# Cross-attention on one core: the next batch's memory blocks move from SP's DMA queue to ScalarE's

## What is computed

```
mp    = memory @ W_mem.T                        # (2048, 1024) a batch
attn  = softmax(x @ mp.T / sqrt(1024))
ctx   = attn @ mp
gate  = sigmoid(concat(x, ctx) @ W_gate.T + b_gate)
out   = rmsnorm(x + gate * ctx) * norm_w
```

## Time and profile before

| what | us |
|---|---|
| median of 3 runs | 1560.95 |
| profiled execution, its own time | 1556.9 |
| its span | 1555.1 |
| PE busy | 1528.3 (98%) |
| DVE busy | 1080.3 (69%) |
| ACT busy | 549.0 (35%) |

### The profile page before, as it was taken

The page is one execution under the profiler, slowest core; times in us unless marked ns, Lnnn a source line. Parts: engine busy times, 40 slices in busy tenths (PEclk is TensorE's granted clock), DMA queues, the critical chain, the costliest instruction groups (busy, mean ns, idle before and its releaser), DMA issues.

```text
span 1555.1 us, 21137 instructions
## 1 busy us (share of the span) xinstructions
PE 1528.3 (98%) x6720; PEld 1262.0 (81%) x6720; DVE 1080.3 (69%) x1502; ACT 549.0 (35%) x919; POOL 33.3 (2%) x72
## 2 busy tenths in 40 slices
PE   7999999999999999999999999999999999999997
PEld 5888888888888878888788888888888888888886
DVE  5654758777777864467446754567555899989987
ACT  4232342222222352244222432234222554444443
POOL 0000000000000000000000000000000001100011
PEclk9999999999999999999999999999999999999999
DMA  9997526333332786757584666757748645555553
GB/s 197 235 241 178 127 88 175 113 113 113 108 108 95 171 214 158 180 142 189 154 208 131 166 166 172 181 139 196 189 133 282 215 181 191 194 197 197 198 198 120
DMA packets 213399, 262.63 MB, mean 169 GB/s; under 512 B 19312, under 2 KB 136048, under 8 KB 213104
## 3 DMA queue, kind: packets, MB, share of 16 engines
q1 hardware_dynamic: 213360, 262.20, 59.8%
HBM read 170.39 MB, written 89.65 MB: 167 GB/s over the span
## 4 chain that ended last, share of the span: by engine, by line
PE 44%; DMA 3%; DVE 1%; issue 1%; ACT 1%; SPq 1%; POOL 0%; ACTq 0%; DVEq 0%; POOLq 0%
PE bank L1604 25%; PE bank L1753 19%; DMA prob_scratch<-prob 2%; DMA region_f<-in_ctx 1%; DMA region_f<-prob_scratch 1%; ACT prob L807 1%; DVE region_l L311 0%; SPq L453 0%; DVE region_n L311 0%; DVE max_part L1232 0%; DVE region_f L1328 0%; SPq L509 0%; ACT region_t L818 0%; ACT region_l L825 0%; POOL mean_sq L693 0%
## 5 line engine op out<-in xcount | busy, mean ns | idle before, releaser
L1604 PE MATMUL bank<-region_n,region_l 128*128 128x512 f32 x1536 | 353.6, 389 | 2.6 <-DVE region_l L311 2.6
L1604 PE MATMUL bank<-region_t,region_l 128*128 128x512 f32 x1536 | 353.7, 389 | 2.2 <-DVE region_l L311 2.1
L1604 PEld LDWEIGHTS bank<-region_t,region_l 128*128 128x128 f32 x1536 | 288.0, 188 | 63.8 <-issue 4.2
L1604 PEld LDWEIGHTS bank<-region_n,region_l 128*128 128x128 f32 x1536 | 288.2, 188 | 63.1 <-DVE region_l L311 2.9
L1604 PE MATMUL bank<-region_t,region_n 128*128 128x512 f32 x960 | 220.2, 392 | 11.6 <-DVE region_t L311 11.6
L1604 PEld LDWEIGHTS bank<-region_t,region_n 128*128 128x128 f32 x960 | 181.4, 189 | 49.9 <-DVE region_t L311 12.0
L825 ACT CAST region_l<-bank 128x512 fp32r<-128x512 f32 x128 | 75.0, 586 | 329.2 <-DVE bank L1261 329.0
L1261 DVE STREAM_TRANSPOSE bank<-region_f 128x512 f32<-128x512 f32 x128 | 88.7, 716 | 102.5 <-DMA region_f<-prob_scratch 100.3
L311 DVE TENSOR_TENSOR region_t<-region_f,region_t 128x1024 fp32r<-128x1024 f32 (+2 forms) x77 | 110.5, 1466 | 67.3 <-ACT region_t L711 60.5
L1645 PE MATMUL bank<-region_t,region_l 128*128 128x512 f32 x576 | 135.7, 389 | 0.0
L1645 PEld LDWEIGHTS bank<-region_t,region_l 128*128 128x128 f32 x576 | 108.1, 188 | 22.4
(11 more groups left out here) (87 smaller groups left out, 1427.6 us busy)
## 6 DMA issues: line engine op xcount, KB each, us to landing
region_f<-in_ctx SPq DMA_DIRECT2D x128, 256.0 KB, 5.6
prob_scratch<-prob SPq DMA_DIRECT2D x128, 256.0 KB, 2.7
region_f<-prob_scratch SPq DMA_DIRECT2D x128, 256.0 KB, 4.3
region_f<-in_x SPq DMA_DIRECT2D x64, 256.0 KB, 6.1
region_f<-in_x SPq DMA_DIRECT2D x128, 128.0 KB, 2.7
region_f<-in_x SPq DMA_DIRECT2D x16, 1024.0 KB, 4.9
out<-region_f SPq DMA_DIRECT2D x31, 512.0 KB, 2.6
q_scratch<-prob SPq DMA_DIRECT2D x8, 1024.0 KB, 6.3
```

Of the source, the lines that this page charges most:

```text
L1604: mm = nc.tensor.matmul(dst, lhs(a), rhs(b), start=first and n == 0, stop=last and n == len(PASSES) - 1)
```

## The change

All loads of the next batch's memory blocks leave SP's stream. ACT issues them, on its own DMA queue: an mt block at the end of a step's work, after `q_split` (steps 1 to 4; in batch 0 steps 2 to 4, two of them after step 2), mn 0 after step 5, mn 1 at the end of step 6, mn 2 in step 7 between the last `pt_split` and the exponentials, mn 3 in step 7 after `q_split`. The split of mn 2 moves: ACT does it at the end of step 7, DVE at the start of step 8. The split of mn 3 moves behind the pieces of step 8. SP's loop over the steps becomes uniform: queries, exchange, store.

```
@@ sync
-            load_next_mt(0, 0)
-            step_sp(2)
-            for j in range(1, MB):
-                load_next_mt(0, j)
-            rest_of_batch(0)
-            with sp.Fori(1, NB - 1) as b:
-                for j in range(MB):
-                    if j < 2:
-                        step_sp(b * UPB + 1 + j)
-                    load_next_mt(b, j)
-                rest_of_batch(b)
+            with sp.Fori(2, (NB - 1) * UPB + 1) as i:
+                step_sp(i)
@@ scalar
+            def next_mt(b, j):
+                act.wait_ge(mn_ready, b * MB)
+                load_mt(act, b, j)
+            def next_mn(b, j):
+                if j == 0:
+                    act.wait_ge(mt_t, b * MTS + MTS)
+                else:
+                    act.wait_ge(mt_ready, b * MTS + HPJ * (j + 1))
+                load_mn(act, b, j)
             def step_act(i, ...):
                 for g in range(MB):
-                    if mn_of is not None and g >= MN_EARLY:
-                        act.wait_ge(av_done, (mn_of * UPB - 1) * MB + g + 1)
-                        mn_split(mn_of, g)
                     pt_split(i, g)
+                if mn_of is not None:
+                    mn_split(mn_of, MB - 1)
+                if mn_next is not None:
+                    next_mn(mn_next, 2)
...
+                if mt_of is not None:
+                    next_mn(mt_of, 1)
                 if mn_next is not None:
-                    for g in range(MN_EARLY):
+                    next_mn(mn_next, 3)
+                    for g in range(MB - 1):
                         act.wait_ge(av_done, (mn_next * UPB - 1) * MB + g + 1)
                         mn_split(mn_next, g)
...
             with act.Fori(1, NB - 1) as b:
-                with act.Fori(1, 6) as u:
-                    step_act(b * UPB + u)
+                for j in range(MB):
+                    step_act(b * UPB + j + 1)
+                    next_mt(b + 1, j)
+                step_act(b * UPB + MB + 1)
+                next_mn(b + 1, 0)
                 rest_of_batch(b)
@@ vector, step_dve
+                if mn_of is not None:
+                    mn_split(mn_of, MN_EARLY)
                 dve.wait_ge(px_loaded, (i + 1) * (16 * NQ))
...
                     pt_split(i, g)
-                    if mn_of is not None and g >= MN_EARLY:
-                        mn_split(mn_of, g)
                 if softmax:
                     unit_max(i + 1)
+                if mn_of is not None:
+                    mn_split(mn_of, MB - 1)
```

More of the change, by code:

```diff
@@ L335, in build, with load_mt, load_mn @@
         NGEV = 6
+        def load_mt(eng, b, j, dst=None):
+            load_quadrants(eng, b_in[j] if dst is None else dst, mem[b, BANK * j:BANK * (j + 1), :], C, mt_loaded[j])
+        def load_mn(eng, b, j):
+            v = b_in[MN_SLOT[j]].rearrange("p (s c) -> p s c", s=TPB)
+            for q in range(NQ):
+                r = M // NQ * q + P * j
+                eng.dma_start(v[SQ * q:SQ * (q + 1)],
+                              mem[b, r:r + P, :].rearrange("(s i) c -> i s c", i=SQ)).then_inc(mn_loaded[j], 16)
         block = ctx.enter_context(nc.Block())
@@ L444, in _ @@
             load_zraw(2, 1)
[L445 to L454, removed]
             sp.wait_ge(w7_ready, W7[S1])
-            load_mt(0, 0, mt0_raw[0])
+            load_mt(sp, 0, 0, mt0_raw[0])
             with sp.Fori(0, NPAIR - 3) as p:
@@ L477, in _ @@
             sp.wait_ge(z_ready, NPROD * NPAIR - 1)
-            load_mt(0, 1)
+            load_mt(sp, 0, 1)
             store_zx(p, 1, slice(0, D), EV_C21, zx_stored[2])
             sp.wait_ge(z_ready, NPROD * NPAIR)
-            load_mt(0, 2)
+            load_mt(sp, 0, 2)
             store_zx(p, 0, slice(BANK, D), EV_C12, zx_stored[1])
             sp.wait_ge(mt_t, HPJ)
-            load_mt(0, 3, mt0_raw[3])
+            load_mt(sp, 0, 3, mt0_raw[3])
             store_zx(p + 1, 0, slice(0, BANK), EV_C11, zx_stored[0])
             sp.wait_ge(mt_ready, HPJ * 2)
-            load_mn(0, 1)
+            load_mn(sp, 0, 1)
             store_zx(p + 1, 1, slice(0, D), EV_C21, zx_stored[2])
@@ L490, in _ @@
             store_zx(p + 1, 0, slice(BANK, D), EV_C12, zx_stored[1])
[L492 to L496, removed]
             def exchange(unit, first=False):
@@ L522, in _ @@
                 sp.wait_ge(zx_stored[i], 16 * NPAIR)
-            load_mn(0, 0)
+            load_mn(sp, 0, 0)
             exchange(0, first=True)
             sp.wait_ge(mt_ready, HPJ * 3)
-            load_mn(0, 2)
+            load_mn(sp, 0, 2)
             sp.wait_ge(mt_ready, MTS)
-            load_mn(0, 3)
+            load_mn(sp, 0, 3)
             def load_q_after_next(i):
@@ L538, in step_sp @@
                 store_am(i)
[L540 to L561, removed]
             sp.dma_start(q_third, q_dram[3]).then_inc(q_first_loaded[3], 16)
@@ L888, in rest_of_batch @@
                 step_act(b * UPB + 8, mn_of=b + 1)
-            with act.Fori(2, 6) as u:
-                step_act(u)
+            step_act(2)
+            next_mt(1, 0)
+            next_mt(1, 1)
+            step_act(3)
+            next_mt(1, 2)
+            step_act(4)
+            next_mt(1, 3)
+            step_act(5)
+            next_mn(1, 0)
             rest_of_batch(0)
             with act.Fori(1, NB - 1) as b:
-                with act.Fori(1, 6) as u:
-                    step_act(b * UPB + u)
+                for j in range(MB):
[3 more added lines that the diff above has]
+                next_mn(b + 1, 0)
                 rest_of_batch(b)
```

## The result

The changed kernel takes 1581.46 us (median of 4 runs, 1581.19 to 1582.14) against 1560.72 before (4 runs). The ratio is 1.0145, 95% interval 1.0133 to 1.0157: slower by 20.7 us. The forecast was 1558.0 in a range of 1557.0 to 1567.0. It was wrong in sign and outside its range. The profiled execution took 1581.58 us with a span of 1579.8, 24.7 more than the span before.

A forecast was written before the change was run, and what follows sets the result against it. PE was taken as the bound, busy for 98% of the span. The terms -2.60 - 0.34 + 0 = -2.94 us took 1560.95 to 1558.0 us; the range of 8 in 10 was 1557.0 to 1567.0.

The forecast's parts named there:

- d = 2.0: Loaded steps of attention: each exchange of weights comes back 2.0 us late, below the 2.8 at which PE stands.
- part (6): Loads running beside the exchange: claimed each exchange late by 2.0 us, between 0 and 5.1, unseen by PE.
- the prize: All PE idle time the change could win back in attention: 2.94 us, 0.19% of the time.
- the five gaps: Late starts of PE ahead of scores phases: 1.07, 0.21, 0.96, 0.13 and 0.57 us.
- Part (1): Splits of mn 2 and 3 leave the pieces of step 8: three late starts close, -2.60 us.
- Part (2): The queue of twelve mt DMAs ahead of the queries' load goes: -0.34 us.
- Part (3): Issuing 32 DMAs a batch on ACT: 0.51 us each, 2.0 a block, in ACT's idle time, no cost to PE.
- Part (4): ACT's waits before mt, mn 0 and mn 1 loads: only a cast queued behind mn 0's, cost nothing.
- The upper bound of 2.7: Exchange beside one block: lateness if the block uses 2.4 us of idle DMA time and otherwise goes first.
- the 5.5 of reserve: Settled step of attention: one exchange can come 5.5 us late before PE stands.
- Rival A: Loaded steps: contention makes every exchange over 2.8 us late, so the kernel is slower, 1562.5 to 1606.6 us; chance 0.20.
- Rival B: Batch crossings only: step 8's pieces or mn 3 late by about 1 us in three batches, 1561.0 us; chance 0.18.

The follow-up runs named there:

- The first experiment: The changed kernel with all loads given back to SP, one block a step, the new order of the splits kept; 1555.36 us, ratio 0.9972 to the kernel before.

## Why the prediction was wrong

**The step that failed** is the cost of the overlap: "d = 2.0" for each loaded step in part (6), with the starts of parts (3) and (4) behind it. It measured 3.5 on average over a batch, 5.1 to 6.0 for mn 0, and 8.5 for the two blocks in one step. The rest of the prediction held, with the exceptions below.

**The bound and the prize: nearly right.** The three versions that keep the exchange clear have none of the five gaps and are faster: 0.9969 to 0.9975, against the 0.9981 of the forecast. The prize was slightly larger than 2.94 us: in the earlier trace rows the phase behind each gap runs 11.01 instead of 10.88 (757.80 - 746.79 in the trace), five times 0.13, so 3.6 in all. The three gain 4 to 5 us by the medians and 1.6 to 2.5 by spans of single profiled executions. What the medians gain beyond 3.6 is not explained: runs of before go from 1556.3 to 1562.7, and its profiled one lies at the low end. The fall of the clock at 583 us comes in some executions and not in others, at 1.6 us in these traces, and can be part of it.

**Part (1), the splits: right.** The first experiment has the crossing as forecast: DVE takes up the weights behind the split of mn 2 at 14.0 to 15.6 (15.1 in the working), and the next exponentials start 9.0 us ahead of the scores phase at 746.90 (7.7 in the forecast, 4.2 before). **Part (2), the queries: right**, by the gaps that stay when mt is bunched.

**Part (3), the issues on ACT: right in size, wrong in place.** Four take 1.8 to 2.0 us. But they do not begin after the queries' cast, 3.4 us behind the first exponential. ACT's queue row stands at 0.2 to 0.5: its DMAs are issued while the exponentials ahead of them in the program are still running, one between two of these. This made the mt blocks cheap, which was luck: nothing in the working counted on it. The prediction feared that SP's issues would lengthen beside them. They did not: three stores took 1.67 us to issue at 659.40, beside ACT's, and 1.67 at 680.78, without.

**Part (4), the waits: where it failed first.** I worked out there, correctly, that mn 0 would be issued between 4.5 and 6.5 us after the exponentials (measured 4.7 to 6.8), and priced it at nothing, since nothing was queued behind it on ACT. I looked at the engine that issues and not at what the DMA engines were doing at that moment. It cost 5.1 to 6.0 us of the exchange. Likewise batch 0's two blocks in one step were priced by ACT's idle time (at most 7.0 in 9.27; their issues took 7.2) and not by the exchange, which they made 8.5 late.

**Part (6), contention: the term mis-sized.** One d of 2.0 us for each loaded step, taken as if all seven steps were mt steps. For a single mt block it was nearly right, 1.7 to 2.9. The sum over steps 1 to 7 of batch 1 is 2.9 + 2.2 + 2.4 + 2.1 + 6.0 + 3.4 + 5.5 = 24.5, so d is 3.5 on average. Step 7's two blocks, priced at up to 5.4, took 4.0 to 5.5. The upper bound of 2.7 from idle engine time was wrong as a bound: it averaged over the exchange, but its last load is one round trip with nothing behind it. My own outer bound of 5.1, one block's time of full engines, is about what a late block costs (4.2 to 6.2 in the version with the later start).

The trace of before already held such a price. The mt blocks bunched on SP run into the exchange of the next step, though they are issued ahead of it, and its weights are back 16.9 us after the exponentials:

```profile
799.52 4.48 SPq L252 DMA_DIRECT2D region_f<-in_ctx  x4
803.31 0.69 ACT L807 ACTIVATE prob<-bank,neg_max 128x512 f32<-128x512 f32 x1 [3.89 <-DVE neg_max L1238]
...
820.25 1.32 DVE L1261 STREAM_TRANSPOSE bank<-region_f 128x512 f32<-128x512 f32 x2 [6.91 <-DMA region_f<-prob_scratch]
```

One such step stays within the 5.5 of reserve; several in a row do not. I read these rows for the queries' load alone.

**Rival A** was what happened. It was given 0.20, and at d = 3.5 it gave 1573. Two terms bring 1581: the double step (3.0), and three falls of the clock behind stalls (4.9), which no part of the prediction had. Not all of its form came true: not every loaded step is over 2.8 late, and not each round trip is stretched, but the first store by an early block and the last load by a late one. For the range I cut off half of A, though by its own working it grew by 3 us for each 0.14 of d.

**Rival B** came as well: the pieces of step 8 are late at 748.29, but as part of A.

The Trainium skill's rule that DMAs of different engines share the same 16 and interleave ("DMA: Bandwidth & Descriptors", Issuing engines are not separate DMA queues) agrees with these runs: a block from SP in the same place makes the exchange 4.8 us late on average, one from ACT 5.2. It was cited for the right fear.

## What to carry to other kernels

Before moving a bulk load to another queue, ask at which moment of the latency-bound transfer it will start, not whether the issuing engine has time. A megabyte that starts with the exchange cost 2 to 4 us of a reserve and, one a step, no time; the same megabyte on its last load cost its full 5. If the dependent transfer signals its landing, one wait on that signal before the bulk load keeps the gain: here it turned 1.0145 into 0.9975.

## What was not expected of the hardware

- ACT's DMAs were issued ahead of activations that stand before them in its program: 0.2 us after the first of four exponentials started, when the last began 2.0 us after it.
- After stalls of 1.9 to 3.8 us PE's granted clock fell to 0.5 in some cases (after 1.90, 2.12, 2.38, 2.86) and not in others (2.45, 2.80, 2.92, 3.17), at about 1.6 us each. A 2.9 us stall can so cost 4.5. What decides is not shown.
- Rows of 512 B or 2 KB made no difference to a single block that started 0.2 to 0.3 us into the exchange (back at 13.7 to 14.3 with either), but at 1.1 to 1.3 it was 15.6 to 15.7 against 14.8, and with two blocks at once 20.1 against 17.6.
